# Row numbers beyond the table's bound for the indirect DMAs of a graph kernel's spare groups

## The reference

```python
def _gin_conv(x, src, dst, n, W1, b1, gamma, beta, W2, b2):
    agg = jax.ops.segment_sum(x[src], dst, num_segments=n)
    h = x + agg
    h = jax.nn.relu(_batchnorm(h @ W1 + b1, gamma, beta))
    return jax.nn.relu(h @ W2 + b2)
...
h = jnp.maximum(_layernorm(x, axis=-1), 0.0)
x = x + ref(h, edge_index, ...)   # batch norm, conv, relu, conv, relu
```

## Time and profile before

| what | value |
|---|---|
| median of 3 runs | 4331.2 us (4330.04 to 4336.28) |
| the profiled execution: its own time | 4327.89 us |
| its span, first to last instruction | 4325.8 us |
| mean granted TensorE clock | 0.79 |
| POOL busy | 3206.3 us (74%), 3352 instructions |
| PE busy | 3209.6 us (74%) |
| DVE busy | 1346.2 us (31%) |
| ACT busy | 494.7 us (11%) |
| DMA packets | 228738, 507.51 MB, mean 117 GB/s |
| bytes on the queue of the indirect DMAs | 436.42 MB |
| bytes on the queue of SP's DMAs | 69.13 MB |

### The profile page before, as it was taken

One profiled execution on the slowest core, in us unless ns is written; L12 is line 12 of the kernel. 1 busy time (PEld: TensorE's weight loads), 2 busy tenths in 40 slices (PEclk: granted clock), 3 DMA queues, 4 the chain that ended last, 5 costly groups with the idle time before them and its releaser, 6 DMA issues.

```text
span 4325.8 us, 29781 instructions
## 1 busy us (share of the span) xinstructions
PE 3209.6 (74%) x9336; PEld 1814.2 (42%) x9336; DVE 1346.2 (31%) x2733; ACT 494.7 (11%) x1296; POOL 3206.3 (74%) x3352
## 2 busy tenths in 40 slices
PE   2777777777777777777787777777777777777767
PEld 2443443444443443334554344443444434444446
DVE  8742344222222222222542222222222222222226
ACT  5300000000000000000470000000000000000016
POOL 3777777777777777777777777777777777777775
PEclk9777777877787778877877777788777787777779
DMA  9233333333333333333463333333333333333349
GB/s 297 85 109 105 103 99 100 105 105 105 105 105 105 105 105 105 105 105 105 147 180 105 105 105 106 105 106 105 106 105 106 105 105 105 105 106 105 106 122 298
DMA packets 228738, 507.51 MB, mean 117 GB/s; under 512 B 57405, under 2 KB 121273, under 8 KB 228579
## 3 DMA queue, kind: packets, MB, share of 16 engines
q0 software_dynamic: 159744, 436.42, 35.1%
q1 hardware_dynamic: 68268, 69.13, 5.0%
q10 hardware_dynamic: 567, 0.00, 0.0%
HBM read 466.84 MB, written 38.49 MB: 117 GB/s over the span
## 4 chain that ended last, share of the span: by engine, by line
POOL 71%; issue 23%; DVE 2%; DMA 2%; PE 1%; ACT 1%; SPq 0%; DVEq 0%; POOLq 0%; ACTq 0%
POOL rows L429 71%; DMA rows<-in_x 1%; DVE bn_stats L852 1%; PE mm_ps L600 1%; ACT acc L641 0%; DVE work L1077 0%; DMA acc<-in_x 0%; DMA rows<-node_rows,edge_ints 0%; DVE acc L1083 0%; SPq L307 0%; DVE bn_mv L864 0%; PE agg_ps L503 0%; SPq L312 0%; PE mm_ps L535 0%; DVE ln_stats L735 0%
## 5 line engine op out<-in xcount | busy, mean ns | idle before, releaser
L429 POOL DMA_INDIRECT rows<-node_rows,edge_ints x3328 | 3186.4, 957 | 1033.0 <-issue 1012.2
L503 PE MATMUL agg_ps<-rows,onehot 128*128 128x257 f32 (+1 forms) x6304 | 2674.7, 529 | 977.8 <-DMA rows<-node_rows,edge_ints 945.6
L503 PEld LDWEIGHTS agg_ps<-rows,onehot 128*128 128x128 f32 x6304 | 1240.4, 239 | 2253.1 <-DMA rows<-node_rows,edge_ints 2124.9
L1003 DVE SCALAR_TENSOR_TENSOR acc<-agg_ps,in_first,acc 128x257 f32 (+1 forms) x394 | 190.9, 485 | 2890.8 <-PE agg_ps L503 2871.0
L897 DVE TENSOR_TENSOR onehot<-dst_all,lane_ps 128x1024 f32<-128x1024 f32 x394 | 476.3, 1209 | 1.5 <-issue 1.5
L690 ACT ACTIVATE acc<-mm_ps,vec 128x128 f32<-128x128 f32 x392 | 122.8, 364 | 2098.2 <-PE mm_ps L535 2098.2
L535 PEld LDWEIGHTS mm_ps<-work,w_a 128*128 128x128 f32 x1568 | 336.9, 298 | 35.0 <-ACT work L684 5.1
L535 PE MATMUL mm_ps<-work,w_a 128*128 128x128 f32 x1568 | 327.7, 380 | 3.1 <-ACT work L684 2.9
L684 ACT COPY work<-tr_ps 128x256 f32<-128x256 f32 x196 | 73.0, 373 | 1597.7 <-PE tr_ps L526 1597.7
L600 PE MATMUL mm_ps<-w_b,work 128*128 128x256 f32 x784 | 181.4, 395 | 37.2 <-ACT work L703 18.8
L1003 DVE SCALAR_TENSOR_TENSOR acc<-agg_ps,in_second,acc 128x257 f32 (+1 forms) x394 | 187.4, 476 | 0.0
(11 more groups left out here) (150 smaller groups left out, 498.7 us busy)
## 6 DMA issues: line engine op xcount, KB each, us to landing
rows<-node_rows,edge_ints POOLq DMA_INDIRECT x3328, 2.7
node_rows<-acc SPq DMA_DIRECT2D x28, 896.0 KB, 6.9
acc<-in_x SPq DMA_DIRECT2D x13, 896.0 KB, 11.9
rows<-in_x SPq DMA_DIRECT2D x13, 896.0 KB, 9.1
out<-acc SPq DMA_DIRECT2D x13, 896.0 KB
acc<-in_x SPq DMA_DIRECT2D x1, 768.0 KB
rows<-in_x SPq DMA_DIRECT2D x1, 768.0 KB
out<-acc SPq DMA_DIRECT2D x1, 768.0 KB
```

The lines of the kernel that those rows point to most:

```text
L429: pool.indirect_dma_start(tile_of(slot, j, D), None, tables[layer][:, :], bass.IndirectOffsetOnAxis(src_all[:, g * G + j:g * G + j + 1], 0 ...
L503: mm = pe.matmul(agg_ps[g % 2][:, 0:width], onehot[:, g % 2, t, :], tile_of(g % R, t, width), start=(t == 0), stop=(t == G - 1))
L1003: dve.scalar_tensor_tensor(to, agg_ps[g % 2][:, 0:width], lanes[:, g:g + 1], to, ALU.mult, ALU.add).then_inc(sums_added, 1)
```

## The change

```diff
+        beyond = sb("beyond", [P, 1])
...
+        rest_marked = sem("rest_marked")
...
-        SETUP_FOLDED = SETUP_LANES + 4 + NC_G + 2
+        SETUP_FOLDED = SETUP_LANES + 5 + NC_G + 2
...
+                    if layer == 0 and g == NGR:
+                        pool.wait_ge(rest_marked, 1)
...
+                        limits = dict(bounds_check=NPAD - 1, oob_is_err=False) if g >= NGR else {}
                         pool.indirect_dma_start(
                             tile_of(slot, j, D), None, tables[layer][:, :],
-                            bass.IndirectOffsetOnAxis(src_all[:, g * G + j:g * G + j + 1], 0)
+                            bass.IndirectOffsetOnAxis(src_all[:, g * G + j:g * G + j + 1], 0), **limits
                         ).then_inc(tile_landed[slot][j], 16)
...
+            setup(dve.tensor_scalar(beyond[:, :], faults[:, :], 0.5, float(NPAD), ALU.is_lt, ALU.mult))
...
+            def mark_rest():
+
+                rest = src_all[:, NGR * G:NG * G]
+                dve.wait_ge(src_ready, 1)
+                dve.tensor_scalar(rest, rest, beyond[:, 0:1], None, ALU.add).then_inc(rest_marked, 1)
...
             begin_walk(0)
+            mark_rest()
             for q in range(NPAIR):
                 measure_pair(q)
```

More of the change, by code:

```diff
@@ L1038, in walk @@
                     if layer == 0:
+                        dve.wait_ge(windows_loaded, 16 * WINDOW_DMAS[0])
                         dve.sem_inc(windows_free, 1)
```

## The result

The changed kernel takes 4317.3 us (median of 10 runs, 4315.2 to 4320.3), the kernel before 4328.8 us on the same chip (10 runs, 4324.2 to 4336.3). The ratio is 0.9974, with a 95% interval of 0.9966 to 0.9982. So it is faster, by 11.5 us; the forecast said 4306 us, 25.2 us less than the 4331.2 us that were shown for the kernel before, so less than half of the forecast gain came. The time lies in the range, between rival B (4315 us) and the partial case (about 4320 us).

The account below looks back on a forecast made before the run. The prediction took POOL's queue of indirect DMAs to bound the kernel. Span 4325.8 + 0.3 (DVE's front) - 0.8 (border) - 24.5 (dense(1)) = 4300.8 us, plus 5.4 gives 4306 us; range 4299 to 4345 us.

Parts of the forecast that it names:

- rival B: In dense(1), store and load limit each other: 290 GB/s a pair, 10 us lost, 4315 us; chance 0.11.
- the partial case: The bounded DMA costs POOL 0.03 to 0.14 us more, part of the gain stays: about 4320 us; chance 0.08.
- the place: dense(1), where spare rows take bandwidth from the loads of x: the place where the change can pay.
- C: Rival: the spare rows move all the same, or equally long transfers replace them; 4331 us as before; chance 0.07.
- D: Rival: the check slows POOL at layer 0's border and its queue's end, deciding from 0.143 us a DMA; chance 0.20.
- e: What a bounded DMA costs POOL more than a plain one; taken at or below 0, ends -0.947 and 0.974 us.
- Faster by more than 0.2%: Whole kernel: time falls by more than 8.7 us, the difference that can't be told from no change; chance 0.70.
- The term of dense(1): In dense(1), without spare rows, loads of x are hardly late, 1.5 us in all: 24.5 us gained.
- The formula for POOL's end: End of layer 1's spare DMAs: span 4300.6 + 176e, wherever this is above what dense(1) leaves.
- The border: End of layer 0: gather(1) starts when the second table has landed, earlier than before; -0.8 us.
- DVE's front: Before walk(0): two added DVE operations stand ahead of the statistics it waits for; +0.3 us.
- From span to time: Whole kernel: 2.1 us from span to profiled execution, 3.3 us more to the median; 5.4 us added.

Follow-up runs that it names:

- e4_load_first: The changed kernel with SP issuing the load of chunk c + 2 ahead of the store of chunk c: 4323.4 us, 0.9968 to the kernel before.

## Why the prediction was right and wrong

Right: the place. The rows were in the way of x in dense(1), all 23 MB went, that stretch became 13.5 us shorter, and the walks kept their pace. The register move is hidden. C is refuted by the bytes. D did not come: e is 0.05 us, under its 0.143, and the kernel with the bound alone is at 0.9997. (D's limit came from the formula of point 2. With that made good it would have been (4325.8 - 4313.8) / 176 = 0.068 us, so the margin was thin.) Faster by more than 0.2% was the likeliest case and came.

Wrong, first the terms of the span in order of size, then the step from span to time:

1. **The term of dense(1)**, 24.5 us forecast, 13.5 measured. The failed step is "a store and a load together are 1.835 MB; at 378 GB/s 4.85 us, and with 1.0 to 1.5 us of fixed time the load has landed 5.85 to 6.35 us after the store's issue". It landed 7.4 us after its own issue, so 7.8 after the store's. The rate was read in a stretch of 6 us at the end and held to be what is left over when the spare rows go. With the rows gone the two pairs above got some 294 GB/s, as the queue falls below 245 GB/s in the course of each pair. Rows 8 had a warning, and the prediction gave it to rival B alone: the stretch from 4262 made 263 GB/s, or 327 for the time its packets were under way. Rival B had the mechanism: with 290 GB/s and 1.5 us of fixed time it has 7.8 us for the pair, as measured, and 10 us of lost time in all (11.8 us of waits in 9 places were measured), but it had a chance of only 0.11. That the load's place behind the store matters I did not weigh at all; e4_load_first showed it.
2. **The formula for POOL's end**, "the span would be 4300.6 + 176e". It leaves out the program's exit. In the kernel before, POOL's drain began 6.4 us after its last DMA's end and took 9.3 us, with 0.2 us to the end behind it. So the formula should have read 4297.9 + 6.4 + 9.3 + 0.2 + 176e, or 4313.8 with e = 0. The drain's row was in the trace of before; I did not read it. By this the forecast span of 4300.8 could not be reached, even with all of the 24.5 us. The floor hardly moved with e: in the changed kernel the spare DMAs of layer 1 end 3.7 us later after the start of dense(1), but the drain begins 3.3 us after the last of them and not 6.4. This is a floor, not a term: in the changed kernel it added 2.1 us, in its repetition nothing that can be told (0.2 us), in the one with the load first 11 us. And it is why the two errors don't add up: with the first one made good, the gain would still have been 12 us.
3. **The border**, -0.8 us forecast, +1.6 measured. "e at or below 0" was wrong in sign, as e is +0.05 us for a DMA whose rows are skipped and for one whose rows move. And the table's landing was not earlier without the rows. The forecast had 3.2 to 3.9 us for the last store "Alone, at 378 GB/s"; the stores of dense(0) land after 4.2 us in the median, where they took 4.4, and the last one after 4.3. The table has landed 92.2 to 92.5 us after PE's first matmul of dense(0) in the kernels without spare DMAs, and the kernel before starts gather(1) at 92.6.
4. DVE's front, +0.3 us forecast: nothing of it can be told from the scatter of the walks (6 us between the four starts of dense(0) above).
5. **From span to time**, 5.4 us forecast. The changed kernel's median is 1.6 us above the profiled span, and over ten runs the kernel before has 3.0 us. This helped the number: the forecast span is 14.9 us too low and the forecast time 11.3 us. It is also why rival B's 4315 us lies so near. Its terms give a span of 4309.3 us, 6.4 us below the measured one, since it lacks the tail and the border and has 2.5 us too much for dense(1). That part of its hit is luck.

On the two rules of the Trainium skill: the measured 0.05 us for 128 row numbers is 0.4 ns each. The 12 cycles an element of "GPSIMD Engine Reference" ("3.1 Elementwise — side-by-side cycle accounting"), an estimate of 1.28 us, is 26 times that, and the measurement decides: that page's section is about elementwise kernels, and its figure does not carry over to a bound checked by the DMA instruction. The other ("DMA: Bandwidth & Descriptors", "Anatomy of one DMA — SWDGE (gpsimd) path") agrees in so far as 128 moved rows or none make no difference to POOL's 1.00 us.

## What to carry to other kernels

Ask of every queue of transfers what stands ahead of the one that is waited for: a load that is needed next goes ahead of a store that nobody needs, and in dense(1) this was worth 6 to 10 us, where taking away the spare rows was worth 10 to 13.5. Before a gain at the end of a kernel is summed, look at each engine's last rows, exits included: the latest of them is a floor, and an engine that only does spare work can be it. Leaving instructions out behind a branch takes away more than making them move nothing, for the instruction's own time, its packets and the late exit all stay. How much more the runs show only roughly: 0.9957 against 0.9974 without the change of order, with intervals that overlap.

## What the runs showed of the hardware

- A bounds-checked indirect DMA of 128 rows with every row out of bounds still puts its 48 packets on the queue, 32 of them with some 16 bytes in place of rows. They hold 2.4% of the engines' time in dense(1), and cost the other transfers nothing that dense(1) shows (100.3 and 100.2 us).
- The bound costs POOL 0.05 us per DMA (0.95 to 1.00 us), rows skipped or not, and a register move of 29 ns that is hidden.
- POOL's drain at the end of the program takes 9.3 us when POOL has first waited for its last indirect DMAs to land (six profiles, drain begun at 4304 to 4312 us). Where POOL does not wait for the last 8 of them, the drain is recorded 7 us ahead of the last DMA's start; it is then 12.2 to 13.1 us long and ends 4.2 to 5.0 us after the last DMA. There it is hidden, with dense(1) still to come. In the two sessions of 5027 us it was 5.3 and 7.9 us in the changed kernel.
- A store and a load of 0.917 MB that SP issues 0.4 us apart move at some 294 GB/s, with dips to 185 to 245 GB/s. Issued behind the store the load lands after 7.4 us, ahead of it after 6.2 us (once 7.3 us).
- In two sessions the kernel before took 16% longer. The kernels with spare DMAs then had dense parts of 168 to 180 us instead of 88 to 114. Leaving the spare DMAs out, with the load first, gave 3.9%; skipping their rows gave nothing. Why the engines stand still there is open.
